# Two-layer graph network: the node update and the next layer's tables as one block pipeline, with centred features

## The chip, the cores and the metric

The kernel runs on one core of a Trainium2 chip. The metric is the device time of one launch in microseconds (us), the median of the runs made.

## The reference

A graph has 6250 nodes of 64 features and 200,000 edges sorted by destination. A first layer (L0) computes an attention over each node's incoming edges and a gated sum, adds it to x and normalises. Then a network of three layers runs. Cut to what matters:

```python
def _ln(x, g, b):
    m = x.mean(-1, keepdims=True)
    v = ((x - m) ** 2).mean(-1, keepdims=True)
    return (x - m) / jnp.sqrt(v + 1e-05) * g + b
...
edge_attr = _mlp(_ln(edge_embed, eng, enb), eW1, eb1, eW2, eb2)
for l in range(3):
    h = _ln(x, n1g[l], n1b[l])
    xi, xj = (h[dst], h[src])
    q = (xi @ Wq[l] + bq[l]).reshape(-1, H, HD)
    kn = (xj @ Wkn[l] + bkn[l]).reshape(-1, H, HD)
    ke = (edge_attr @ Wke[l] + bke[l]).reshape(-1, H, HD)
    ...                                      # vn, ve alike
    alpha = (q * (kn + ke)).sum(-1) / scale  # softmax over the edges of a node
    msg = ((vn + ve) * alpha[..., None]).reshape(-1, D)
    agg = jax.ops.segment_sum(msg, dst, num_segments=n)
    gate = jax.nn.sigmoid(agg @ Wih[l] + bih[l] + h @ Whh[l] + bhh[l])
    upd = agg + gate * (h @ Wself[l] + bself[l] - agg)
    x = x + upd @ Wout[l] + bout[l]
    h2 = _ln(x, n2g[l], n2b[l])
    x = x + _mlp(h2, mW1[l], mb1[l], mW2[l], mb2[l])
return _ln(x, ng, nb)
```

The result is added to the network's input and normalised once more, `_layernorm(x + ...)`. Of the next layer's h only the mean-free part of x is used; the last norm too takes the mean away.

## The kernel before, in words

All waits and orders are written out by hand: each engine has one program, and semaphores that the text names tie them. The stages follow each other in time:

- **Opening.** SP issues the loads. A loop over seven groups builds the node table `tab0`: SP loads features (`load_features`, L340), PE turns and multiplies (L645, L649), ACT copies, SP stores (`store_tables`, L402). POOL meanwhile gathers blocks of `dst` (L552), then gathers chunk 0 from `tab0` (L546), then scatters `s2exp` (L565).
- **First pass.** 28 chunks of 128 x 56 edges. POOL gathers 56 rows a chunk (L546) with one indirect DMA for each, in seven groups of eight; DVE runs the scans of L0's attention; PE and ACT run the edge network in seven steps a chunk, four 512-column products each way (L689, L696). From the second group on POOL holds until PE has finished a step of the chunk before (`m_pe`). ACT copies a chunk's states once a chunk (L910).
- **Tables of a layer (L728 to L745, L952, L1391 to L1412).** Node features lie turned, two nodes' 64 features on 128 partitions, in 3200 columns: six blocks of 512 columns and one of 128 (`BLK`, `NB` = 7). Each operation runs over all seven blocks before the next: mean (PE, L726), centre (DVE, L1379), square (ACT, L939), mean square (PE), Ln (L946) and Exp with scale -0.5 (L950), product and scale (L1384, L1387), projection (PE, L744) and biases (DVE, L1409 and L1411). SP stores `tabkv` block by block, then all of h and of the queries; POOL scatters the queries into `qexp`, 49 indirect DMAs of 128 nodes (L599), as soon as a block is ready.
- **Edge pass of a layer.** 28 chunks; POOL gathers keys and values (L546), 56 a chunk; DVE scans; ACT copies states to S1 and stores them.
- **Node update (L761 to L806, L992 to L1007, L1472 to L1519).** POOL fetches the final edge state of each node (L588, 49 DMAs). Blocks go in two halves (`HALVES`: blocks 0 to 2, then 3 to 6). In a half each operation runs over all its blocks before the next: `sums`, turn, copy, gate, self, mix, out, the second norm, four hidden products with Relu, the folded product, and the addition to x.
- **End.** The last two norms, operation by operation over all blocks, turned back and stored.

SP's queue between node update and tables: it waits for the end of the node update (L516), issues the 30 loads of the next layer's node weights (L457 to L469), stores x, then stores tables; then come source indices, edge features and the next table weights (L480 to L499). POOL's first gather of a layer waits for the indices (`idx1`), for `a_out` and for `h_out`.

## Time and profile before

| | us |
|---|---|
| runs (three) | 9158.19, 9160.3, 9160.95 |
| median | 9160.3 |
| profiled execution: its own time | 9160.98 |
| its span | 9159.2 |
| busy: PE, DVE, ACT, POOL | 3667.0, 5799.7, 2862.4, 6365.8 |

The span is the time from the first to the last instruction in the profile. Busy time is the sum of an engine's instructions; issuing a plain DMA and waiting are not counted. A row of waits says which engine stood still in front of which line, and what ended the wait.

### The profile page before, as it was taken

To read this page: it belongs to the slowest core of one execution; us is meant where nothing else is said; L and a number is where in the kernel's file an instruction comes from. 1 tells how busy PE (TensorE), PEld (TensorE's weight loads), DVE (VectorE), ACT (ScalarE), POOL (GpSimd) and SP (SyncE) were. 2 spreads that over 40 slices of the span, in tenths; PEclk is the share of its full clock that TensorE was granted. 3 is DMA by queue.
4 is the path that set the end of the run, shared out by engine and by line. 5 is a ranking of instruction groups with operands and counts; after the bars stand their busy time and mean duration, and the time that the engine had idled before them with its cause. 6 is when DMAs were issued, how large, how long until landed. Compare 5 with 4: busy or idle time off the path is not lost.

```text
span 9159.2 us, 45368 instructions
## 1 busy us (share of the span) xinstructions
PE 3667.0 (40%) x9857; PEld 2190.5 (24%) x9857; DVE 5799.7 (63%) x6114; ACT 2862.4 (31%) x2181; POOL 6365.8 (70%) x6734
## 2 busy tenths in 40 slices
PE   2677777776323233223342232322242222223325
PEld 1333333333122122212121221222222122212212
DVE  1666666666366776676437667767744776677673
ACT  0566666666122222222222222222221222222223
POOL 6677777774577777777457777777736777777762
PEclk9988888888656566555666665665576656656557
DMA  3455555554433443444234334434314443444331
GB/s 52 161 192 180 186 179 174 175 184 148 132 131 131 139 149 131 139 140 141 64 108 148 132 132 141 147 131 139 125 49 138 139 149 131 137 141 141 131 110 48
DMA packets 405487, 1247.08 MB, mean 136 GB/s; under 512 B 196101, under 2 KB 253910, under 8 KB 360006
## 3 DMA queue, kind: packets, MB, share of 16 engines
q0 software_dynamic: 215104, 429.19, 17.4%
q1 hardware_dynamic: 169606, 468.24, 14.6%
q10 hardware_dynamic: 20736, 349.23, 9.5%
q14 instruction: 31, 0.25, 0.0%
q8 instruction: 10, 0.16, 0.0%
HBM read 808.34 MB, written 437.84 MB: 136 GB/s over the span
## 4 chain that ended last, share of the span: by engine, by line
POOL 52%; issue 20%; PE 17%; ACT 7%; DVE 2%; DMA 1%; DVEq 1%; ACTq 0%; POOLq 0%; SPq 0%
POOL G L546 49%; PE PS L696 7%; PE PS L689 6%; ACT S L910 4%; POOL qexp L599 1%; PE PS L777 1%; POOL QQ L588 1%; PE PS L781 1%; ACT hid L886 1%; PE PS L666 1%; POOL s2exp L565 1%; POOL S L552 1%; POOL G L588 1%; ACT S L851 0%; ACT L855 0%
## 5 line engine op out<-in xcount | busy, mean ns | idle before, releaser
L546 POOL DMA_INDIRECT G<-tabkv,srcI x4704 | 4438.4, 944 | 1433.6 <-issue 1433.6
L756 PE MATMUL PS<-Wkvp,EA 128*128 128x256 f32 x4704 | 1672.9, 531 | 4296.3 <-DVE PX L1438 4217.8
L756 PEld LDWEIGHTS PS<-Wkvp,EA 128*128 128x128 f32 x4704 | 1253.4, 274 | 4716.5 <-DVE PX L1438 4381.7
L546 POOL DMA_INDIRECT G<-tab,srcI x1568 | 1481.4, 945 | 571.9 <-issue 507.2
L959 ACT ACTIVATE QQ<-QQ 128x3584 f32<-128x3584 f32 x84 | 538.4, 6410 | 3313.5 <-DVE PX L1438 3063.1
L1435 DVE TENSOR_TENSOR PS<-PS,G 128x512 f32<-128x512 f32 x588 | 408.4, 695 | 1593.3 <-DMA G<-tabkv,srcI 1575.3
L973 ACT ACTIVATE S<-SX 128x4480 f32<-128x4480 f32 x81 | 663.7, 8194 | 1238.4 <-DVEq L1462 1238.4
L689 PE MATMUL PS<-xT,W1p 128*128 128x512 f32 x1568 | 768.5, 636 | 252.2 <-ACT xT L847 243.1
L1424 DVE TENSOR_TENSOR_SCAN QQ<-PS,QQ 128x456 f32<-128x456 f32 x672 | 679.4, 1082 | 207.9 <-ACT QQ L959 192.3
L1461 DVE TENSOR_TENSOR_SCAN SX<-PS,SX 128x456 f32<-128x456 f32 x756 | 763.2, 1082 | 12.2
L696 PE MATMUL PS<-hid,W2p 128*128 128x512 f32 x1568 | 710.9, 596 | 34.2 <-ACT hid L886 31.5
L1438 DVE TENSOR_TENSOR PX<-PS,QQ 128x512 f32<-128x512 f32 x588 | 624.6, 1062 | 43.8
L886 ACT ACTIVATE hid<-PS,b1c 128x512 f32<-128x512 f32 x784 | 489.1, 684 | 300.6 <-PE PS L689 300.6
L1454 DVE TENSOR_TENSOR SX<-G,PS 128x3584 f32<-128x3584 f32 x84 | 525.7, 6258 | 87.8 <-ACT PS L968 87.8
L689 PEld LDWEIGHTS PS<-xT,W1p 128*128 128x128 f32 x1568 | 318.7, 205 | 660.4 <-issue 396.8
L1436 DVE TENSOR_TENSOR G<-PS,G 128x512 f32<-128x512 f32 x588 | 399.4, 679 | 0.0
L696 PEld LDWEIGHTS PS<-hid,W2p 128*128 128x128 f32 x1568 | 284.4, 190 | 342.0 <-issue 227.7
L910 ACT ACTIVATE S<-S 128x7336 f32<-128x7336 f32 x27 | 360.5, 13352 | 0.0
L599 POOL DMA_INDIRECT qexp<-PX,startI x147 | 140.9, 958 | 312.2 <-DVEq L1412 268.3
L1441 DVE TENSOR_REDUCE al<-PX 128x448 f32<-128x3584 f32 x84 | 326.6, 3888 | 7.7
L666 PE MATMUL PS<-ident,xe 128*128 128x128 f32 x784 | 132.0, 296 | 363.0 <-DVE xe L1188 363.0
L894 ACT ACTIVATE eaC<-PS,b2c 128x512 f32<-128x512 f32 x196 | 134.7, 687 | 418.8 <-PE PS L696 418.8
(311 smaller groups left out, 4090.8 us busy)
## 6 DMA issues: line engine op xcount, KB each, us to landing
st<-S ACTq DMA_DIRECT2D x81, 2240.0 KB, 7.8
EA<-eaT SPq DMA_DIRECT2D x84, 1792.0 KB, 7.8
QQ<-qexp SPq DMA_DIRECT2D x84, 1792.0 KB, 7.3
st<-S ACTq DMA_DIRECT2D x27, 3668.0 KB, 12.0
G<-tabkv,srcI POOLq DMA_INDIRECT x4704, 2.5
xe<-in_edge_attr SPq DMA_DIRECT2D x28, 1792.0 KB, 8.1
qexp<-zeros SPq DMA_DIRECT2D x28, 1792.0 KB, 12.6
eaT<-eaC ACTq DMA_DIRECT2D x28, 1792.0 KB
```

What stands on the lines that cost most here:

```text
L546: nc.gpsimd.indirect_dma_start(out=G[:, u, t, :], out_offset=None, in_=tab[:, :], in_offset=IND(ap=srcI[:, u, t:t + 1], axis=0)).then_inc( ...
L689: last = mm(PS[:, 1 + 2 * r + kh, :], W1p[:, r, kh, :], xT8[:, :], start=True, stop=True)
L696: last = mm(PS[:, 5, :], W2p[:, kh, r, :], hid8[:, r, kh, :], start=(r == 0 and kh == 0), stop=(r == 1 and kh == 1))
L756: last = mm(PS[:, b + j // 2, 2 * P * (j % 2):2 * P * (j % 2) + 2 * P], EA[:, u, 4 * s + j, :], Wkvp[:, :], start=True, stop=True)
L886: f(hid8[:, r, kh, :], PS[:, 1 + 2 * r + kh, :], ACT.Relu, bias=b1c[:, kh:kh + 1]).then_inc(m_act, 1)
L910: f(S0r[:, :, :], SY[:, :, 1:CX].rearrange("p r c -> p c r"), ACT.Copy).then_inc(s0_rows, 1)
L959: f(Qf[:, :, 1:CX], Q1.rearrange("p c d -> p d c"), ACT.Copy).then_inc(q_flat, 1)
L973: f(S1[:, :, :], SX[:, :, 1:CX].rearrange("p r c -> p c r"), ACT.Copy).then_inc(s_rows, 1)
L1424: scan(rows, gate8f, rows, 0.0, ALU.mult, ALU.add)
L1438: tt(PR[:, steps, :], kv_of(b)[:, :, 0:D], Qf[:, :, 1 + 8 * s:9 + 8 * s].rearrange("p d t -> p t d"), ALU.mult).then_inc(kv_used, 1)
L1454: tt(SX[:, 2 * H:R1, 1:CX].rearrange("p (j h) x -> p j h x", h=H), G1[:, u, :, D:2 * D].rearrange("p t (h d) -> p d h t", h=H), score8[:, ...
L1461: scan(rows, gate8f, rows, 0.0, ALU.mult, ALU.add)
```

## The change

The node update of a layer, the next layer's tables (or, after the last layer, the two last norms) become one list of steps. Each step has a position; block k's step of position d stands at 8k + d (`SKEW` = 8), and each engine issues its own steps in that order (`in_turn`). So several blocks are under way at once.

The features x are kept centred: x is centred once at the start with `Cmat` (identity minus the mean matrix), and `Wout`, `mW2` and their biases are centred once a layer (`centred_weights`), so that the sums stay mean-free, and the two mean products and centrings in each block's norms go. The inverse root, Ln and Exp on ACT, becomes Sqrt on ACT and a reciprocal on DVE (`scaled_by_spread`). The product of h with `Whh` is computed for all blocks ahead of the pipeline, and the gate product adds to it. Projections are done and handed over in quarters of a block.

On SP's queue the node weights of layer 0 and the weights of the last norm are loaded in the opening, before the loop that builds `tab0`; those of a later layer are loaded behind its table stores. h, x and the queries are stored block by block. `x1` is loaded for the end into S1. The layer loop runs twice, and the last layer is written out behind it. In the first pass POOL holds from the third group on, one step earlier.

```diff
+TILES = NPR
+SKEW = 8
+def in_turn(depth):
+    order = sorted((SKEW * k + d, k, step) for k in range(NB) for step, d in depth.items())
+    return [(k, step) for _, k, step in order if not (step.startswith("project") and int(step[-1]) * P >= BLK[k][1])]
...
+        NODE_PE = {"turn": 1, "gate": 3, "self": 5, "out": 7, "spread2": 10, "hidden0": 12, "hidden1": 14, "hidden2": 16,
+                   "hidden3": 18, "fold": 20}
+        NODE_ACT = {"agg": 2, "gate": 4, "square2": 9, "root2": 10.5, "relu0": 13, "relu1": 15, "relu2": 17, "relu3": 19}
+        NODE_DVE = {"sums": 0, "mix": 6, "onto": 8, "norm": 11, "onto2": 21}
+        TABLE_PE = {"spread": 23, "project0": 25, "project1": 25.5, "project2": 26.5, "project3": 27.5}
+        TABLE_ACT = {"square": 22, "root": 23.5}
+        TABLE_DVE = {"h": 24, "project0": 26, "project1": 26.5, "project2": 27.5, "project3": 28.5}
+        LAST_PE = {"spread": 23, "y_centre": 25, "y_spread": 27, "y_turn": 29}
+        LAST_ACT = {"square": 22, "root": 23.5, "y_square": 26, "y_root": 27.5}
+        LAST_DVE = {"y": 24, "y_norm": 28, "y_copy": 30}
+
+        def bank_of(k, j):
+            return k - 1 if k > 0 and j % 2 == 1 else k
...
             edge_weights(0)
             table_weights(0)
+            node_weights(0)
+            for q in range(2):
+                for j, name in ((NGC, "ng"), (NBC, "nb")):
+                    sp.dma_start(cb[q * D:(q + 1) * D, j:j + 1], A[name].unsqueeze(1), allow_slow_non_contiguous=True).then_inc(c_x, 16)
...
+            def store_tables1(m):
+
                 for k in range(NB):
-                    hold(sp, waits_sp, a_dve, l * A_DVE + 2 * NB + k + 1)
+                    hold(sp, waits_sp, projection_used, m * TILES + tiles_to(k))
...
+                if last:
+                    hold(sp, waits_sp, st1_out, (l + 1) * (16 * (NCH + 1)) + 16)
+                    sp.dma_start(nX1, x1Td[:, :]).then_inc(c_x, 16)
+                else:
+                    edge_weights(l + 1)
+                    store_tables1(l + 1)
+                    node_weights(l + 1)
...
-                        if k > 0:
-                            hold(pool, waits_pool, m_pe, 28 * (2 * i + u - 1) + (4 * k - 3 if k > 1 else 0))
+                        if k > 1:
+                            hold(pool, waits_pool, m_pe, 28 * (2 * i + u - 1) + (4 * k - 7 if k > 2 else 0))
...
+                    j = int(step[-1])
+                    if j == 0:
+                        hold(pe, waits_pe, h_ready, m * NB + k + 1)
+                    elif j == 1:
+                        hold(pe, waits_pe, projection_used, m * TILES + max(4 * k, 1))
+                    else:
+                        hold(pe, waits_pe, projection_used, m * TILES + 4 * k + (j - 1 if k > 0 else j))
+                    mm(PS[:, bank_of(k, j), 0:6 * D], nH[:, c0 + j * P:c0 + (j + 1) * P], Wqkv[:, :],
+                       start=True, stop=True).then_inc(projected, 1)
...
-                    f(nB4[:, c0:c0 + w], PS[:, k, 0:w], ACT.Ln, bias=epsc[:, 0:1]).then_inc(ln_ready, 1)
...
-                    f(nB4[:, c0:c0 + w], nB4[:, c0:c0 + w], ACT.Exp, scale=-0.5).then_inc(done, 1)
...
+            for k in range(NB):
+                c0, w = BLK[k]
+                act.wait_ge(x0_centred, k + 1)
+                f(nX[:, c0:c0 + w], PS[:, k, 0:w], ACT.Copy)
+                f(nB3[:, c0:c0 + w], PS[:, k, 0:w], ACT.Square).then_inc(squared, 1)
+            for k in range(NB):
+                root(k, 0)
...
+            def scaled_by_spread(k, dst, g_, b_):
+
+                c0, w = BLK[k]
+                cols = slice(c0, c0 + w)
+                v.reciprocal(nB4[:, cols], nB4[:, cols])
+                settle()
+                tt(nB5[:, cols], nX[:, cols], nB4[:, cols], ALU.mult)
+                settle()
+                return ts(dst[:, cols], nB5[:, cols], cb[:, g_:g_ + 1], cb[:, b_:b_ + 1], ALU.mult, ALU.add)
...
+                elif step == "y_norm":
+                    dve.wait_ge(y_rooted, k + 1)
+                    v.reciprocal(nB4[:, cols], nB4[:, cols])
```

## Rows read from the trace of the kernel before

**Rows 1.** Windows, one boundary: us, then busy PE, PEld, DVE, ACT, POOL, clock, DMA

```profile
4547.00:4651.00 104.00, 87.65 (x220) 41.11 (x220) 43.14 (x79) 46.41 (x75) 0.40 (x2) 0.90 0.06 20
...
sum 230.00, PE 128.04 PEld 62.44 DVE 71.28 ACT 59.51 POOL 96.22; mean PE 42.68 PEld 20.81 DVE 23.76 ACT 19.84 POOL 32.07
```

**Rows 2.** List of waits, whole span: us in total, times, longest

```profile
DVE PS L1435 <- DMA G<-tabkv,srcI: 1575.3, 252, 8.4
...
POOL qexp L599 <- DVEq L1412: 268.3, 3, 103.6
...
POOL G L546 <- PE PS L696: 57.8, 34, 17.1
```

**Rows 3.** Chain that ended last, in order of time: start, us, what

```profile
1340.88 13.26 ACT S L910
...
1413.41 13.28 ACT S L910
...
4471.95 4.08 DMA st<-S
...
4611.53 11.21 PE PS L781 x32
...
8943.84 4.08 DMA st<-S
```

**Rows 4.** Timeline at the first boundary: start, us, engine, line

```profile
4495.57 0.20 DVE L1483 TENSOR_SCALAR QQ<-QQ 128x64 f32<-128x64 f32 x1 [13.47 <-DMA QQ<-st,endI]
...
4497.72 1.09 PE L766 MATMUL PS<-ident,PX 128*128 128x128 f32 x4 [23.33 <-DVEq L1490]
...
4623.76 1.12 SPq L361 DMA_DIRECT2D cb<-in_bself  x2
...
4642.27 0.42 SPq L471 DMA_DIRECT2D xTd<-G  x1
...
4714.07 0.96 POOL L546 DMA_INDIRECT G<-tabkv,srcI  x1 [0.30 <-issue]
```

**Rows 5.** Opening: timeline, the table stores' line, and their landing

```profile
27.97 0.43 SPq L383 DMA_DIRECT2D bqkv<-in_bve  x1
...
35.84 0.40 SPq L340 DMA_DIRECT2D xe<-in_x  x1
...
95.69 0.94 POOL L546 DMA_INDIRECT G<-tab,srcI  x1 [0.30 <-issue]
...
L402 SPq DMA_DIRECT2D tab<-xe x7: 388/390/422, 41.4 to 88.0; - x7
...
tab<-xe SPq DMA_DIRECT2D x7, 458.5 KB, 4.5
```

**Rows 6.** Timeline of one chunk of the first pass

```profile
1355.57 0.23 DVE L1208 TENSOR_TENSOR al<-G,ewC 128x56 f32<-128x56 f32 x1
...
1366.06 0.94 POOL L546 DMA_INDIRECT G<-tab,srcI  x1 [2.84 <-PE PS L696]
```

**Rows 7.** DVE groups by form, 4484 to 4672: busy us, mean ns, idle before

```profile
L1379 DVE TENSOR_TENSOR EA<-G,PS 128x512 f32<-128x512 f32 x12 | 7.7, 682 | 0.6 <-PE PS L726 0.5
...
L1485 DVE RECIPROCAL QQ<-QQ 128x64 f32<-128x64 f32 x6 | 3.3, 552 | 0.4
...
L1387 DVE TENSOR_SCALAR EA<-EA,cb 128x512 f32<-128x512 f32 x6 | 3.3, 546 | 0.5
...
L1485 DVE RECIPROCAL QQ<-QQ 128x8 f32<-128x8 f32 x1 | 0.2, 202 | 0.1
```

**Rows 8.** A table load by form (mean ns); PE's busy time and clock

```profile
L946 ACT ACT_TABLE_LOAD x3 | 3.8, 1283 | 0.1
...
9117.00:9122.00 5.00, 0.16 (x2) 0.99 0.00 0
9122.00:9127.00 5.00, 4.31 (x5) 0.50 0.01 2
```

**Rows 9.** POOL's query scatters: duration ns, first and last start

```profile
L599 POOL DMA_INDIRECT qexp<-PX,startI x147: 954/958/986, 2414.6 to 6947.3; - x147
```

More of the change, by code:

```diff
@@ L747, in _, with edges1 @@
+            def edges1(l):
+                hold(pe, waits_pe, projection_used, (l + 1) * TILES)
                 with pe.Fori(0, NCH // 2) as i:
@@ new lines, in _ @@
+            pe.wait_ge(a_x, 16)
+            hold(pe, waits_pe, l_t, 16 * NTW)
+            for k in range(NB):
+                c0, w = BLK[k]
+                mm(PS[:, k, 0:w], Cmat[:, :], nX[:, c0:c0 + w], start=True, stop=True).then_inc(x0_centred, 1)
+            for k, step in in_turn(TABLE_PE):
+                table(k, step, 0)
+            with pe.Fori(0, L - 1) as l:
+                edges1(l)
+                hold(pe, waits_pe, l_t, (l + 2) * (16 * NTW))
+                for k, step in in_turn({**NODE_PE, **TABLE_PE}):
+                    if step in NODE_PE:
+                        node(k, step, l)
+                    else:
+                        table(k, step, l + 1)
@@ new lines, in _ @@
+            edges1(L - 1)
+            for k, step in in_turn({**NODE_PE, **LAST_PE}):
+                c0, w = BLK[k]
+                if step in NODE_PE:
+                    node(k, step, L - 1)
+                elif step == "spread":
+                    table(k, step, L)
+                elif step == "y_centre":
+                    pe.wait_ge(h_ready, L * NB + k + 1)
+                    mm(PS[:, k, 0:w], Cmat[:, :], nB5[:, c0:c0 + w], start=True, stop=True).then_inc(y_centred, 1)
+                elif step == "y_spread":
+                    pe.wait_ge(y_squared, k + 1)
+                    mm(PS[:, k, 0:w], onesD[:, :], nB3[:, c0:c0 + w], start=True, stop=True).then_inc(y_spread, 1)
+                else:
+                    pe.wait_ge(y_normed, k + 1)
+                    for j in range(w // P):
+                        last = tr(PS[:, k, j * P:(j + 1) * P], nB5[:, c0 + j * P:c0 + (j + 1) * P], ident[:, :])
+                    last.then_inc(y_turned, 1)
@@ new lines, in square, with root @@
+            def square(k, m):
+                c0, w = BLK[k]
+                act.wait_ge(x2_ready, (m - 1) * NB + k + 1)
+                f(nB3[:, c0:c0 + w], nX[:, c0:c0 + w], ACT.Square).then_inc(squared, 1)
+            def root(k, m):
+                c0, w = BLK[k]
+                act.wait_ge(spread, m * NB + k + 1)
+                f(nB4[:, c0:c0 + w], PS[:, k, 0:w], ACT.Sqrt, bias=epsc[:, 0:1]).then_inc(rooted, 1)
+            for k in range(NB):
+                c0, w = BLK[k]
+                act.wait_ge(x0_centred, k + 1)
+                f(nX[:, c0:c0 + w], PS[:, k, 0:w], ACT.Copy)
+                f(nB3[:, c0:c0 + w], PS[:, k, 0:w], ACT.Square).then_inc(squared, 1)
@@ L955, in query, with layer @@
+            for k in range(NB):
+                root(k, 0)
+            def layer(l):
                 def query(n):
@@ L1413, in _, with layer @@
+            biases(0)
+            for k, step in in_turn(TABLE_DVE):
+                table(k, step, 0)
+            def layer(l):
                 v.memset(gate8[:, :, 0:1], 0.0)
@@ L1492, in mix @@
-                def mix(k, c0, w):
-                    stt(nB4[:, c0:c0 + w], PS[:, k, 0:w], cb[:, BSELF:BSELF + 1], nB2[:, c0:c0 + w], ALU.add, ALU.subtract)
+                centred_weights(l)
+            with dve.Fori(0, L - 1) as l:
+                layer(l)
+                biases(l + 1)
+                for k, step in in_turn({**NODE_DVE, **TABLE_DVE}):
+                    if step in NODE_DVE:
+                        node(k, step, l)
+                    else:
+                        table(k, step, l + 1)
```

446 lines of the change are left out of this document (221 added, 225 removed).

## The prediction

> **What bounds the kernel now.** I read the windows by stage first [rows 1]. At the boundary between two layers POOL first fetches the 49 groups of final edge states; from 4547 to 4651 it then does nothing (0.40 us busy) while PE is busy 88 of 104 us; and up to 4714 it scatters the 49 query groups. The list of waits names the hole: POOL waited three times, 268 us in all and 104 us at the longest, for the DVE step that ends the first table block (L1412) [rows 2]. Once the first attention gather is out at 4714, POOL issues without a pause, and DVE waits for it; so the start of the gathers sets the end of each layer's edge pass. Layers repeat every 2236 us (8943.84 against 4471.95) [rows 3]. What the change can win at the two boundaries between layers is therefore an earlier first gather than 4714.07 [rows 4]; at the end of the program, an earlier last block; in the opening, where the chain that ended last runs through one POOL issue after another, every microsecond that POOL starts later is lost [rows 5].
>
> In the first pass one chunk takes 72.5 us (one L910 to the next) [rows 3]. POOL's 56 gathers at 1.25 us take 70 and then POOL waits: 2.84 us in the chunk shown, 57.8 us over the pass, always for PE [rows 6, 2].
>
> **The first pass.** The released group goes out 8 gathers, 10 us, earlier, and the next group then waits for the same product. DVE uses the gathered rows at 1355.57 after waiting for ACT (L910), not for a gather [rows 6], and no wait of DVE on a gather of this pass is in the list. PE and ACT set the 72.5 us. Cost 0, bounds -3 and +3 (other DMA traffic beside them). The work that hides it is that PE and ACT chain; without it POOL's wait of at most 58 us would be the price.
>
> **The opening.** 30 loads of node weights and 4 of the last norm move ahead of the feature loop on SP's queue. SP is idle from 28.4 to 35.8 [rows 5]. In the old place the 30 take 18.5 us (4623.76 to 4642.27) [rows 4]; 4 more make 21, so SP is free at about 49.5 and not before 35.84. The table stores ran from 41.4 to 88.0 and landed 4.5 us later, 92.5; the first gather at 95.69 waited for nothing [rows 5], a slack of 3. Shifting the second feature load by 13.6 and following the loop's hand-overs (load lands, turn, product, store, landing), the last store shifts by 9.5 to 11, so the gather starts 7 us late. Bounds 3 and 13. Also one DVE subtraction of 128 columns before the one-hot sums, 0.2. I take +7.
>
> **Table stage 0.** ACT now copies and squares all seven blocks from PSUM, loads one table (1.28) [rows 8] and takes roots; DVE then needs a reciprocal, a product and a scale. The Exp pass over all blocks and its own table load are gone. Block 0 is ready at about 2409.6 against 2414.6 [rows 9]; DVE then needs 9 us a block against POOL's 10.1 us for eight scatters, so POOL stays the bound and keeps those 5 us. I take -5, bounds -8 and +3.
>
> **The reciprocal** is the largest added work: Exp(-0.5 Ln) on ACT becomes Sqrt on ACT and a reciprocal of up to 512 columns on DVE. The trace has none wider than 64: 202 ns for 8 columns, 552 for 64 [rows 7], a slope of 6.25 ns a column. Linearly a block costs 0.55 + 448 x 0.00625 = 3.35 us; scaled in proportion it costs 8 x 0.552 = 4.4. I take 3.35, since the two rows show a fixed part, and keep 4.4 for the range. The Trainium skill (VectorE: DVE Perf Modes, on why there are eight slices) says the reciprocal iterates with a repeat count of 8; an estimate from that is 4.3 us plus the fixed part for a block, the upper of the two ends. By it the sum would be some 45 us worse; the two rows' slope is below it, so I don't take it.
>
> **DVE's load.** At a boundary it did 71 us [rows 1]. Two centrings a block go (12 x 0.68 = 8 us) [rows 7], two reciprocals come (6.25 block equivalents x 2 x 3.35 = 42), and projection goes in quarters, 8 small additions a block for 4 (+4, my estimate): 109 us, 17.4 a block and with the added drains 18.5. PE: 16 products (each two records) over three blocks of 512 columns and one of 128 in 11.21 us [rows 3]: 0.86 us for 512 columns at full clock. Each block keeps 13 such, four projections (2.6) and four turns (0.9): 14.6 us. ACT was busy 59.5 us a boundary [rows 1], 9.5 a block, and loses more than it gains: not the bound. It loads a table twice a window, because Sigmoid (position 4) lies between the roots (10.5 and 23.5, that is 2.5 and 7.5 of a window). The Trainium skill (ScalarE: Activation LUTs, the table of advice) says to do all functions of one table set before switching and gives about 2.7 us a load; the row says 1.28 [rows 8]. By 2.7 each window would grow by up to 3 us; the row decides.
>
> **The pipeline's window.** Engines run in order, so I walked the written order (8 positions a window) with these durations. In a full window DVE does h of block k-3 (3.35, a drain of 0.08, product and drain 0.77, scale 0.55 [rows 7]: 4.75), onto, sums (2.15: 4495.57 to PE's turn at 4497.72 [rows 4]): 7.6. Then PE turns block k (1.1), projects, and spreads block k-1, which ends at 11.2; root at 11.95; DVE's second norm to 16.75; two quarters and onto2 to 19.0; mix to 21.2; and the next window's root, behind square, spread and a table load, is done at 22.3. So DVE works 18.5 of 22.3, and what it waits for is the turn and spread in front of the second norm and the root at the window's end. PE stands still about 4.3 us, works 0.7, and stands 2.1 more before the turn. After a stillness of 5.1 us its granted clock went from 0.99 to 0.50 for the next 5 us [rows 8], which would add 2.1 to the path; I take 1.5, hence 23.8, bounds 18.6 (DVE's work alone) and 29 (PE's 14.6 at half clock).
>
> **A boundary.** The first sums start at 4495.57 as before. The first three windows, when a block's 24 dependent steps pass one by one, take 12.5, 17 and 17, and 4 for the slow clock: 50, to 4545.6. Then 27 (block 0's projections all share one bank), 24, 24, 22, 17, 9 and 5: the last block is ready at about 4673.5. Rows come every 10.2 us, faster than windows, so they hide; POOL's eight scatters (10.1) also fit a window, and the last ones end near 4681. What is late next is SP: only after the last block's four stores (1.9) does it issue the 30 node weights (18.5), and behind these stand the source indices (2.4 with landing), which POOL's first gather waits for. 4673.5 + 22.8 = 4696.3 against 4714.07: -17.7 each, -35 for two. The 19 table weights and the query load stand behind on SP, some 11 us after the first gather, hidden by DVE's waits for gathers (1575 us in 252 waits [rows 2]). If that cover were gone: 11 us a layer. Bounds of a boundary: -49 with windows of 18.6, +16 with windows of 30.
>
> **The end.** The first sums come at 4495.57 + 4471.9 = 8967.5. Windows hold y (5.5), the second norm (4.75) and y_norm (4.1), whose reciprocals all stand in one chain (y, centre, square, spread, root, y_norm, turn, then self and mix): 26.8, with clock 28. 8967.5 + 50 + 28 + 28 + 28 + 25 + 18 + 13.5 + 8.5 = 9166.5, and 2.8 for the last store: 9169.3 against 9159.2, +10. Bounds -27 and +50. Covers: loads of x1 and the last norm are done before the sums.
>
> **Sum.** 7 + 0 - 5 - 35 + 10 = -23. The profiled run took 9160.98 with a span of 9159.2, and the median is 9160.3, so the forecast is 9137.
>
> **Rivals.**
> *The clock holds* and the waits overlap as the order intends: 1.5 off each window and 4 off each fill: about -30 a boundary and -2 at the end: 7 - 5 - 60 - 2 = -60, 9100. For it: with PE busy 84% of the time the clock was 0.90 [rows 1]. Against it: the stillness of 5.1 us [rows 8]. If windows shrink to DVE's own 18.6 it would be 7 - 5 - 98 - 27 = -123, 9037; against that speaks the chain walked above.
> *The reciprocal costs 4.4*, the other side: 2.1 more a window, five and a half windows at each boundary, 3.2 in some six at the end, 45 us in all: +22, 9182. It decides from windows 1.5 us longer than I take (25.3): 15 of them eat the 23. Unseen hand-overs of that size do the same.
> *PE becomes the bound at half clock*: 29 us of products a block; boundaries +16, end +50: +84, 9244. Against it: PE busy 84% had a clock of 0.90 [rows 1], and a PE that lags is busy throughout.
> *The change doesn't bring the gathers forward*, because SP's weights stand before the indices: that is already in the sum at 18.5; without it 9100.
>
> **Chances.** Forecast's own case 0.38, its range 9115 to 9160; clock holds 0.20; windows near DVE's work 0.10; reciprocal or hand-overs dearer 0.22; PE at half clock 0.10. About 0.2%, 18 us, is what this measurement can tell from no change. Faster: 0.30 and 0.24 of the first case, 0.54; within: 0.14 and half of the fourth, 0.25; slower 0.21. The range leaves out PE at half clock (0.10), half of the windows near DVE's work (0.05) and the worst of the fourth case (0.05): 9070 to 9195. It holds 9100 and 9182, so both signs.
>
> **What would show it.** The new reciprocals' mean for 512 columns (3.35). First gather of the chunks at about 102.5, of a layer at about 2480 and 4700, and what it waits for: SP's indices, not scatters. First sums to last projection 178 us. SP's node weights right behind the last block's stores. Clock in the windows 0.7 to 0.9. First-pass chunk 72.5 us with POOL still waiting 2.8. Wrong would make it: windows outside 22 to 26 us, or an opening that moves by other than 7.

## The result and the profile after

The changed kernel takes 9175.6 us (median of 20 runs, 9171.3 to 9180.0), the kernel before 9161.0 beside it (20 runs): a ratio of 1.0016, 95% interval 1.001 to 1.0022. The forecast was 23 us faster; it is 15 us slower, and the interval leaves no doubt of the sign, though the time is inside the range of 9070 to 9195. The profiled run has a span of 9171.6 us, 12.4 more than before.

Where the 12.4 us come from is read off the chain that ended last (start, us, what): the last state store of each edge pass ends a stretch.

```profile
2282.90 5.76 DMA st<-S
...
4480.90 4.08 DMA st<-S
...
6710.41 4.11 DMA st<-S
...
8938.50 4.09 DMA st<-S
```

Two of the same rows of before stand in [rows 3], the other two are:

```profile
2276.39 5.82 DMA st<-S
...
6708.12 4.10 DMA st<-S
```

The differences:

| stretch | before | after | change | forecast |
|---|---|---|---|---|
| opening and first pass | 2276.4 | 2282.9 | +6.5 | +7 |
| table stage 0 and layer 0's edge pass | 2195.6 | 2198.0 | +2.4 | -5 |
| boundary 1 and layer 1's edge pass | 2236.2 | 2229.5 | -6.7 | -17.7 |
| boundary 2 and layer 2's edge pass | 2235.7 | 2228.1 | -7.6 | -17.7 |
| last node stage and norms | 215.4 | 233.1 | +17.7 | +10 |

**The opening**, in the timeline (start, us, engine, line, what it waited for); it answers to the first gather of [rows 5]:

```profile
102.96 0.94 POOL L593 DMA_INDIRECT G<-tab,srcI  x1 [7.38 <-DMA tab<-xe]
```

POOL starts 7.3 us later and now waits for the stores of the first table. From there to the last state store it takes 2179.9 us, before 2180.7: the first pass neither gains nor loses.

**Table stage 0**, timeline of the first two blocks:

```profile
2400.31 3.35 DVE L1461 RECIPROCAL EA<-EA 128x512 f32<-128x512 f32 x1 [14.89 <-ACT EA L1018]
...
2405.20 1.62 PE L818 MATMUL PS<-Wqkv,G 128*128 128x384 f32 x2 [6.36 <-DVE G L1465]
...
2413.97 1.91 PE L809 MATMUL PS<-G,onesD 128*128 128x512 f32 x2
...
2415.72 0.99 POOL L646 DMA_INDIRECT qexp<-PX,startI  x1 [55.69 <-DVEq L1516]
2415.93 0.69 ACT L1018 ACTIVATE EA<-PS,epsc 128x512 f32<-128x512 f32 x1 [15.65 <-PE PS L809]
2416.65 3.35 DVE L1461 RECIPROCAL EA<-EA 128x512 f32<-128x512 f32 x1 [1.80 <-ACT EA L1018]
...
2427.68 0.96 POOL L646 DMA_INDIRECT qexp<-PX,startI  x1 [2.12 <-DVEq L1516]
```

The first scatter is 5.4 us earlier in its stretch than before ([rows 9]: 2414.6 - 2276.4 against 2415.7 - 2282.9). But block 1's variance product (L809) stands in PE's queue behind block 0's four projections, so its root comes only at 2415.93, and the next blocks follow every 11 to 12 us, not every 10.1. POOL waits 1 to 2.3 us before each of them, and its first gather of the layer comes 204.0 us after the state store, not 201.4.

**The first boundary.** What is ready when is read off POOL's waits for the last quarter of each block (timeline; in brackets POOL's idle time):

```profile
4577.45 0.98 POOL L646 DMA_INDIRECT qexp<-PX,startI  x1 [21.76 <-DVEq L1516]
4607.07 0.96 POOL L646 DMA_INDIRECT qexp<-PX,startI  x1 [19.78 <-DVEq L1516]
4631.53 0.96 POOL L646 DMA_INDIRECT qexp<-PX,startI  x1 [14.47 <-DVEq L1516]
4652.95 0.95 POOL L646 DMA_INDIRECT qexp<-PX,startI  x1 [11.45 <-DVEq L1516]
4671.03 0.95 POOL L646 DMA_INDIRECT qexp<-PX,startI  x1 [8.11 <-DVEq L1516]
4686.88 0.95 POOL L646 DMA_INDIRECT qexp<-PX,startI  x1 [6.07 <-DVEq L1516]
```

Its start, one full window and its end:

```profile
4502.64 0.56 PE L840 MATMUL PS<-cb,Cmat 128*128 128x2 f32 x2 [19.31 <-DMA G<-xTd]
...
4504.51 0.25 DVE L1475 TENSOR_SCALAR QQ<-QQ 128x64 f32<-128x64 f32 x1 [0.66 <-DMA QQ<-st,endI]
...
4510.36 0.60 PE L776 MATMUL PS<-ident,PX 128*128 128x128 f32 x4
...
4511.73 1.10 PE L780 MATMUL PS<-G,Wn 128*128 128x512 f32 x2 [0.78 <-ACT G L993]
...
4586.24 3.35 DVE L1461 RECIPROCAL EA<-EA 128x512 f32<-128x512 f32 x1 [1.53 <-ACT EA L1018]
...
4593.88 1.09 PE L776 MATMUL PS<-ident,PX 128*128 128x128 f32 x4 [1.87 <-DVEq L1482]
...
4596.04 1.91 PE L801 MATMUL PS<-EA,mW1s 128*128 128x512 f32 x2
...
4597.74 1.62 PE L789 MATMUL PS<-G,onesD 128*128 128x512 f32 x2
...
4610.84 3.35 DVE L1461 RECIPROCAL EA<-EA 128x512 f32<-128x512 f32 x1 [1.53 <-ACT EA L1018]
...
4691.07 0.28 DVE L1515 TENSOR_TENSOR PX<-PS,bqkv 128x128 f32<-128x128 f32 x1
...
4693.94 1.11 SPq L392 DMA_DIRECT2D cb<-in_bself  x2
...
4713.70 0.35 SPq L522 DMA_DIRECT2D srcI<-in_src  x1
...
4716.37 0.96 POOL L593 DMA_INDIRECT G<-tabkv,srcI  x1 [17.14 <-DMA srcI<-in_src]
```

From one h to the same step of the next block it is 24.6 us; in it PE's products cost double after its stillness (1.91 for 512 columns, 1.02 later), and the windows (us; busy PE, PEld, DVE, ACT, POOL; granted clock; DMA share, GB/s) say that DVE works 16.8 of the 24.6 us:

```profile
4586.20:4610.80 24.60, 17.86 (x39) 7.65 (x38) 16.78 (x22) 9.12 (x13) 3.92 (x4) 0.86 0.15 40
```

After the last block SP issues the node weights from 4693.9 on, then the source indices at 4713.70, and POOL has waited 17 us for them. That part of the forecast holds. The reciprocal's own line (duration min/median/max):

```profile
L1461 DVE RECIPROCAL EA<-EA x49: 953/3353/3355, 2400.3 to 9162.6; 128x512 f32<-128x512 f32 x42, 128x128 f32<-128x128 f32 x7
```

3.35 us for 512 columns, the slope of the two narrow rows of [rows 7].

### The profile page after: what moved, and what is told of

It reads as the page before. It is cut to its first block, busy times and chain, and to the rows that moved or that the text cites. A ratio compares the mean times of both kernels' runs of the same rounds, so it can differ in the third digit from the quotient of the medians.

```text
span 9171.6 us, 44763 instructions
## 1 busy us (share of the span) xinstructions
PE 3660.6 (40%) x9779; PEld 2159.1 (24%) x9779; DVE 5951.5 (65%) x6211; ACT 2909.8 (32%) x2189; POOL 6367.4 (69%) x6734
## 4 chain that ended last, share of the span: by engine, by line
POOL 50%; issue 19%; PE 17%; ACT 7%; DVE 4%; DMA 1%; SPq 1%; DVEq 1%; ACTq 0%; POOLq 0%
POOL G L593 49%; PE PS L743 7%; PE PS L736 6%; ACT S L964 4%; DVE EA L1461 1%; PE PS L818 1%; PE PS L801 1%; ACT hid L940 1%; PE PS L713 1%; POOL s2exp L612 1%; POOL G L635 1%; ACT S L905 0%; ACT L909 0%; DMA G<-xTd 0%; PE PS L793 0%
## 5 line engine op out<-in xcount | busy, mean ns | idle before, releaser
L833 PE MATMUL PS<-Wkvp,EA 128*128 128x256 f32 x4704 | 1633.4, 520 | 4239.4 <-DVE PX L1575 4163.4
L833 PEld LDWEIGHTS PS<-Wkvp,EA 128*128 128x128 f32 x4704 | 1222.3, 267 | 4651.5 <-DVE PX L1575 4333.8
```

The costliest lines, as they stand in the source:

```text
L833: last = mm(PS[:, b + j // 2, 2 * P * (j % 2):2 * P * (j % 2) + 2 * P], EA[:, u, 4 * s + j, :], Wkvp[:, :], start=True, stop=True)
```

## Experiments

All medians stand beside runs of the kernel before on the same chip; changes in us are against the changed kernel's 9175.6 unless said otherwise. "Stretch" is the time between two of the state stores above, in the profiled run. Of the small steps, three (the opening, the variance product, the two banks) have ratios whose intervals overlap with the interval of the kernel they vary: there the trace carries the argument, and the size in the median is uncertain by some us.

### The opening alone

```diff
             table_weights(0)
-            node_weights(0)
...
             sp.wait_ge(a_x, 16)
+            node_weights(0)
```

> The changed kernel with the 30 node weights and the 4 loads of the last norm issued where the table stage begins (after x has landed) and not in the opening. Theory: they hold SP's second feature load back, so POOL's first gather comes at 103 and not at 96; everything behind it in the first pass is a chain of POOL, PE and ACT, so the time falls by those 6.5 us, to 9169, and SP is free again at about 2411, before the first table block is ready at 2415. Rival: the first pass swallows a late start (it is not bound by POOL alone), and the time stays at 9175.6 within 2 us. Second rival: in the new place they stand ahead of the first block's stores and cost there what they give back: first gather of the first layer later by up to 10 us, time 9169 to 9180.

Measured: 9167.9 (ratio 1.0007, 0.9998 to 1.0016), 7.7 less; in the profiled run the first stretch is 5.3 shorter. The first gather is back:

```profile
95.90 0.94 POOL L593 DMA_INDIRECT G<-tab,srcI  x1 [0.30 <-issue]
```

The opening's term was right, in size and in mechanism, and the new place costs nothing: the next stretch is 2198.1 us, 2198.0 in the changed kernel.

### The first pass's gathers alone, on the kernel before

```diff
-                        if k > 0:
-                            hold(pool, waits_pool, m_pe, 28 * (2 * i + u - 1) + (4 * k - 3 if k > 1 else 0))
+                        if k > 1:
+                            hold(pool, waits_pool, m_pe, 28 * (2 * i + u - 1) + (4 * k - 7 if k > 2 else 0))
```

> The kernel before with one part of the change alone: the gathers of the first pass are released one step of the product further ahead. Theory: PE and ACT set the 72.5 us of a chunk, POOL waits for PE anyway, so nothing: 9161 within 3 us. Rival: the earlier gathers give back POOL's waits of 57.8 us or part of them (9105 to 9155), or crowd the other transfers of the pass (9165 or more).

Measured: 9160.4 against 9160.4 (ratio 1.000, 0.999 to 1.0009). Nothing, as forecast.

### Table stage 0: variance product ahead

```diff
-            for k, step in in_turn(TABLE_PE):
+            for k, step in in_turn({**TABLE_PE, "spread": 16}):
```

> The changed kernel, in the first table stage alone: PE does the variance product of block k+1 before the projections of block k and not behind them. Theory: the root of the next block stands behind the four projections, so a block takes 11.4 to 12.1 us where POOL's eight scatters take 10.1; with the product ahead DVE never waits for a root and POOL goes from block to block without a pause: waits of 2.1, 1.9, 1.2, 1.0 and 2.3 us go, about 7 in all, and the time falls by 5 to 8 us, to 9169. Rival: DVE's own work and the four projections that share a bank (2.5 us each at the lower clock) set the period, then the time falls by less than 2 us.

Measured: 9166.2 (ratio 1.0007, 0.9998 to 1.0016), 9.5 less; in the profiled run the stretch falls from 2198.0 to 2192.2, 5.8 less, and POOL's waits fall to at most 1.1 us. The whole profiled span is only 3.7 shorter. So the 5 us that the forecast had here existed; a place in PE's queue took them.

### Source indices ahead of the node weights

```diff
                 for u in range(2):
                     queries(u)
+                node_weights(l)
...
                     store_tables1(l + 1)
-                    node_weights(l + 1)
```

> The changed kernel with each layer's 30 node weights issued on SP behind that layer's first two query loads (so neither in the opening nor between the last table block and the source indices); the four loads of the last norm go where the table stage begins. Theory: at a boundary POOL's first gather waits 17 us for source indices that stand behind 18.9 us of weights; with the indices in front, POOL waits for its own scatters and the fetch of the boundary queries, which end at about 217 us after the last state store, and the gathers start at 218 to 220 and not at 234: 15 to 17 us at each of two boundaries, and the opening's 7.7 on top: 9175.6 - 7.7 - 32 = 9136. Rival: the weights now stand before the third chunk's indices, or the query load (14 us behind the first gather already) becomes what DVE waits for; then DVE starts as late as before, and less than 8 us a boundary is kept: 9152 to 9168.

Measured: 9139.2 (ratio 0.9976, 0.9966 to 0.9986), 36.4 less. The boundary stretches fall by 16.9 and 13.4, as much as the first gather moves (from 235.5 and 234.0 us after the last state store to 218.4 and 220.6); the rest is the opening. POOL goes from its last scatter through the boundary queries to the gathers without a wait. The query load is issued only at 4708.13, 14 us behind the first gather, and costs nothing, since the stretch shrinks as much as the gather moves:

```profile
4690.01 0.35 SPq L521 DMA_DIRECT2D srcI<-in_src  x1
...
4692.56 0.99 POOL L648 DMA_INDIRECT qb<-tabq,firstI  x1 [0.30 <-issue]
...
4693.85 0.97 POOL L592 DMA_INDIRECT G<-tabkv,srcI  x1 [0.30 <-issue]
```

So the node weights on SP's queue (18.9 us here, 18.5 in the sum) are a real price and an avoidable one, and without them the change is faster than the kernel before.

### The products with Whh inside each gate step

```diff
-                    mm(... Wn[:, 1, :], nB2[:, cols], start=False, stop=True ...)
+                    mm(... Wn[:, 2, :], nH[:, cols], start=True, stop=False)
+                    mm(... Wn[:, 1, :], nB2[:, cols], start=False, stop=True)
...
-                for k in range(NB):
-                    mm(PS[:, k, 0:w], Wn[:, 2, :], nH[:, c0:c0 + w], start=True, stop=False, ...)
```

> The changed kernel with the product of h and Whh back in each block's gate step (two products in a row), and the wait for the reloaded h and x in front of the first of them and no longer in front of the bias product. Theory: at each of the three node stages the first turn waited for 7.4 us of products that themselves waited for the reload; now the first sums are no longer held up by the copy of the bias (about 1 us) and the turn follows them at once: first turn 3.7 us earlier, the last block too, 3.7 us at each of two boundaries and at the end: -11, 9165. Rival: the added product in every window lies on the path (turn, project, spread) at 0.9 to 1.9 us and eats this: 0 to +10 us, 9176 to 9186.

Measured: 9174.8 (ratio 1.0016, 1.0007 to 1.0025), 0.8 less. The first turn did come earlier, and the gain was gone three rows later:

```profile
4504.66 1.09 PE L776 MATMUL PS<-ident,PX 128*128 128x128 f32 x4 [22.87 <-DVEq L1481]
...
4506.80 2.05 PE L782 MATMUL PS<-G,Wn 128*128 128x512 f32 x2 [1.05 <-ACT G L992]
4508.64 1.91 PE L783 MATMUL PS<-G,Wn 128*128 128x512 f32 x2
```

The seven products in front had left PE at full clock (the gate product of block 0 took 1.10); without them turn, gate and self each run at the lower clock, beside the added product. My theory, that the late first turn costs each stage 3.7 us, falls: the second norm of block 0 starts 45.9 us after the state store here and 45.2 in the changed kernel.

### Block 0's projections in two banks

On the run just told: its last bank stays unused until late, so block 0 can alternate.

```diff
-            return k - 1 if k > 0 and j % 2 == 1 else k
+            return (k - 1) % NB if j % 2 == 1 else k
```

> The changed kernel with the gate's two products in a row (as in the run of that part), which leaves the last block's PSUM bank unused until late, and block 0's second and fourth projection in that bank, so that block 0 alternates two banks as the others do. Theory: the step from block 0 ready to block 1 ready took 29.6 us where the later ones take 24.5 and I had 24; it is the four projections one after another through one bank (2.4 us each), and with two banks 5 us go at each boundary, 2 in the first table stage and 3 at most at the end, which has no projections: 9174.8 less 12: 9163. Rival: block 1's window is long for another reason (its turn and root pass while three blocks still fill the pipeline), and the time stays within 3 us of 9174.8.

Measured: 9174.4, but where the kernel before takes 9171.9: ratio 1.0003 (0.9994 to 1.0012), 0.13% or 12 us below the ratio of the run it builds on, with intervals that overlap. In the traces the first gathers of the two boundaries come 7.1 and 4.3 us earlier after the state store than in that run. The step from block 0 to block 1:

```profile
4577.90 0.99 POOL L646 DMA_INDIRECT qexp<-PX,startI  x1 [20.85 <-DVEq L1513]
4602.22 0.96 POOL L646 DMA_INDIRECT qexp<-PX,startI  x1 [13.85 <-DVEq L1513]
```

24.3 us, where the changed kernel has 29.6 and the run this one builds on 29.0. What the one bank costs is not only that its four projections pass one by one at the lower clock. In the changed kernel DVE's addition that frees it stands behind a second norm:

```profile
4569.18 3.35 DVE L1461 RECIPROCAL EA<-EA 128x512 f32<-128x512 f32 x1 [3.44 <-ACT EA L1002]
...
4574.65 1.23 PE L818 MATMUL PS<-Wqkv,G 128*128 128x384 f32 x2 [4.72 <-DVEq L1516]
...
4580.69 0.75 DVE L1498 SCALAR_TENSOR_TENSOR G<-PS,cbc,G 128x512 f32<-128x512 f32 x1 [4.16 <-PE PS L793]
```

PE stands still 4.7 us before block 0's fourth projection, the folded product behind it (L793) is late, and DVE then waits 4.2 us for that. With two banks neither wait is there, and from h of block 0 to h of block 1 it is 24.8 us in place of 31.1 (30.5 in the run it builds on).

### The load of x1 at the end

```diff
+                    sp.wait_ge(rows_got[3], (L + 1) * 128)
                     sp.dma_start(nX1, x1Td[:, :]).then_inc(c_x, 16)
...
-            dve.wait_ge(c_x, 80)
...
                 elif step == "y":
+                    if k == 0:
+                        dve.wait_ge(c_x, 80)
```

> The changed kernel, at the end of the program alone: the load of x1 (11.5 us) is issued only after 32 of the 49 groups of final states have been fetched, and DVE waits for it before the first y and no longer before the first sums. Theory: at the end the first sums come 26.8 us after the last state store, at the boundaries 23.6; the difference is this load, so 3 us come back: 9172.5. Rival: the later load is missed by y of block 0 (78 us after the last state store) or the 3 us are taken up by the first windows: 9175 or more.

Measured: 9176.7 (ratio 1.0017, 1.0008 to 1.0026), no gain. The first sums came 23.8 us after the last state store and not 26.8, but the first turn stayed at 29.9: PE comes to it at 8971.47, straight from the products with Whh that it began at 8963.95, so it waits for those and not for the sums. The theory falls; the late sums were real and covered.

### Without the wide reciprocals

```diff
-                v.reciprocal(nB4[:, cols], nB4[:, cols])
-                settle()
                 tt(nB5[:, cols], nX[:, cols], nB4[:, cols], ALU.mult)
```

> The changed kernel without the wide reciprocals of the layer's two norms and of the first last norm (what they should have turned into a factor is multiplied as it is; 41 of the 48 wide reciprocals and their drains are left out, those of y_norm stay). It prices the reciprocal by what its absence gives back. Theory: both stand in the chain of a window (h, turn, spread, root, norm), so a window of 24.6 us loses 2 x 3.4 and takes 18: 5.5 windows a boundary, 35 to 40 us each, 35 to 45 at the end, 10 or less in the first table stage, in all -110 to -130: 9045 to 9065. Rival: PE's 14.6 us at full clock (up to 22 at a lower one) and ACT's table loads take over as the bound, and less than 60 us come back: above 9115.

This leaves out the 42 wide and 7 narrow reciprocals of L1461. Measured: 9038.8 (ratio 0.9865, 0.985 to 0.988), 136.8 less; its four runs lie between 9033.9 and 9049.7. The profiled one is the longest of them, and there the boundaries are 35.9 and 32.7 shorter, the end 49.1, the table stage 6.5. At the first boundary blocks follow every 18.4 to 18.9 us, 6 less than 24.6 for 6.7 us of reciprocals left out. They stand in the chain almost whole.

### PE kept busy while DVE forms h

```diff
                     if j == 0:
+                        hold(pe, waits_pe, rooted, m * NB + k + 1)
+                        for _ in range(4):
+                            mm(PS[:, k, 0:w], onesD[:, :], nB3[:, c0:c0 + w], start=True, stop=True)
                         hold(pe, waits_pe, h_ready, m * NB + k + 1)
```

> The changed kernel with four more products of 512 columns in front of each block's first projection, where PE stands still while DVE forms h (their result is overwritten; nothing is left out). Theory: PE's stillness of 4.3 us lets the granted clock fall, and turn, projection, hidden product and variance product behind it then take twice as long (1.09, 1.49, 1.91 and 1.62 us); kept busy, PE runs them at full clock and a window loses 2 to 3 us: 5.5 windows at each of two boundaries: 22 to 33 us less, 9143 to 9154 (the end has no projections and no added products). Rival: the clock is no term of the window, or the 3.4 us of added products get in the way of turn and variance product: the same time within 5 us, or up to 20 more.

Measured: 9167.0 where the kernel before takes 9171.9: ratio 0.9994 (0.9985 to 1.0003), 0.22% or 20 us below the changed kernel's ratio. The full window, from h to h:

```profile
4583.60:4605.70 22.10, 18.82 (x48) 7.87 (x46) 16.79 (x23) 9.13 (x12) 4.50 (x5) 1.00 0.17 46
```

Here the granted clock is 1.00 in place of 0.86 and the window 22.1 in place of 24.6, with more work in it. The added products do not hold the clock everywhere: of the two such full windows at each boundary, one has it lower all the same.

```profile
4605.70:4631.00 25.30, 21.68 (x48) 9.32 (x46) 16.84 (x23) 9.13 (x12) 7.85 (x8) 0.87 0.21 62
...
6811.10:6836.00 24.90, 21.65 (x48) 9.31 (x46) 16.79 (x22) 9.13 (x12) 3.53 (x4) 0.86 0.15 39
6836.00:6858.50 22.50, 18.80 (x47) 7.88 (x46) 16.84 (x22) 9.12 (x12) 7.85 (x8) 1.00 0.24 70
```

With the same instructions a window takes 22.1 and 22.5 us at 1.00, and 25.3 and 24.9 at 0.87 and 0.86: the lower clock costs 2.4 to 3.2 us of a full window; I had taken 1.5. More of the gain comes at the end of the pipeline: the two steps from h to h after 4656.72 take 18.4 and 12.7 us in the changed kernel at a clock of 0.81 and 0.73, here 15.8 and 11.0 at 1.00. The start gives some of it back (h of block 0 comes 1.8 and 1.6 us later), and the last quarter comes 5.9 and 3.3 us earlier after the state store than in the changed kernel. In the table stage, where the same products stand, POOL waits once, for 0.8 us, and the first gather comes 196.1 us after the state store in place of 204.0 (stretch 2194.2 for 2198.0).

### Another order in the window

```diff
-        NODE_PE = {"turn": 1, ..., "spread2": 10, ...}
-        NODE_ACT = {"agg": 2, ..., "square2": 9, "root2": 10.5, ...}
-        NODE_DVE = {"sums": 0, "mix": 6, "onto": 8, "norm": 11, "onto2": 21}
+        NODE_PE = {"turn": 0.5, ..., "spread2": 8.8, ...}
+        NODE_ACT = {"agg": 0.7, ..., "square2": 8.3, "root2": 8.95, ...}
+        NODE_DVE = {"sums": -0.6, "mix": 6, "onto": 7.8, "norm": 9.5, "onto2": 21}
```

> The changed kernel with another written order inside the window: DVE does sums and onto before h of the block three behind (then the second norm before the quarters), PE turns and spreads before the projections, ACT squares, copies and takes the root before the relu. Nothing is added or left out. Theory: the window of 24.6 us is a chain (h 4.75 us on DVE, then turn and variance product on PE at the lower clock, then root, then the second norm), not DVE's work of 18.5; with sums covering the output product and h covering turn, spread and root, a window takes 19 to 20.5 us. Five and a half windows a boundary: 22 to 28 us each, and some 20 at the end, so 9100 to 9115 in all. Rival: PE at the lower clock (29 us a block) or ACT's two table loads set the window; then it stays above 23 and the time falls by less than 20 us.

Measured: 9124.3 (ratio 0.9962, 0.9949 to 0.9976), 51.4 less with the same instructions. The boundaries gain 10.9 and 10.5, less than expected, the end 26.9. h and the second norm now follow each other without a wait (timeline), and the window is 22.6 us at a clock of 0.92:

```profile
4579.74 3.34 DVE L1461 RECIPROCAL EA<-EA 128x512 f32<-128x512 f32 x1
...
4584.39 3.34 DVE L1461 RECIPROCAL EA<-EA 128x512 f32<-128x512 f32 x1
...
4602.37 3.34 DVE L1461 RECIPROCAL EA<-EA 128x512 f32<-128x512 f32 x1
```

```profile
4579.70:4602.30 22.60, 17.01 (x40) 7.27 (x38) 16.74 (x23) 8.90 (x12) 7.69 (x8) 0.92 0.24 70
```

The window of the changed kernel was a chain and not DVE's work, as the forecast had walked it; what the forecast did not draw from its walk is that another written order would shorten the chain.

### The three parts together, and variants

The order above, the indices first and the variance product ahead:

> The changed kernel with three of the parts above together: source indices ahead of the node weights (which also clears the opening), the first table stage's variance product ahead of the projections, and the new order inside the window. Theory: they sit in different places (SP's queue, the first table stage, the windows), so their gains add: 36.4 and 9.5 and 51.4 us off 9175.6, 9078. Rival: they share a bound. With blocks ready earlier POOL's own scatters (10.1 us for eight) and the fetch of the boundary queries end last, or the query load that stands behind the gathers is missed; then a boundary keeps less than 20 of its 27 us and the time is 9090 to 9110.

Measured: 9088.5 (ratio 0.9922, 0.9909 to 0.9936), 87 less than the changed kernel where the medians add to 97. The profiled spans add nearly exactly: 33.7, 3.7 and 49.2 off 9171.6 is 9085.0, measured 9086.7. The median lies between the theory's 9078 and the rival's 9090; the boundaries keep 24.6 and 23.1 us.

With a second order (gate, self and mix beside h and the norm, fold earlier, sums and two quarters later):

```diff
+        NODE_PE = {"turn": 0.5, "gate": 0.9, "self": 1.45, "out": 2.5, "spread2": 8.8, "hidden0": 10.45, ..., "fold": 18.4}
+        NODE_DVE = {"sums": -4, "mix": 2.05, "onto": 6, "norm": 9.5, "onto2": 19}
+        TABLE_DVE = {"h": 24, "project0": 26, "project1": 26.5, "project2": 28.2, "project3": 28.4}
```

> As the run with the three parts together, with a second written order of the window: gate and self of the new block and then mix stand beside h and the second norm, fold comes right behind hidden3, sums and the last two quarters behind onto2. Nothing is added or left out. Theory: in the window of 22.6 us DVE still waited 2.8 us for fold, 1.3 for out, 1.0 for self and about 2 for quarters; with the order walked through by durations DVE has one wait of 1 to 2 us left and a window takes 18.5 to 20. 2.6 to 4 us off some 17 windows: 45 to 65 us less than the other run. Rival: PE, in order too, now waits for DVE in front of products that were ready (self and out behind the projections), and the window does not get shorter: within 15 us of the other run, or slower.

Measured: 9113.9 (ratio 0.9948, 0.9935 to 0.9962), 25 more than the run with the three parts. Both theories saw half: blocks follow every 18.6 to 20.9 us and not 20.2 to 24.1, but the first is ready 103.7 us after the state store and not 93.2, and the end takes 239.7 us and not 207.6. The boundary stretches are 1.3 and 3.9 us shorter, so the whole loss is at the end.

With the factors formed on ACT as before the change:

```diff
-                f(nB4[...], PS[:, k, 0:w], ACT.Sqrt, bias=epsc[:, 0:1]).then_inc(rooted, 1)
+                f(nB4[...], PS[:, k, 0:w], ACT.Ln, bias=epsc[:, 0:1]).then_inc(ln1, 1)
+                act.wait_ge(ln1, m * NB + k + 1)
+                f(nB4[...], nB4[...], ACT.Exp, scale=-0.5).then_inc(rooted, 1)
```

> As the run with the three parts together, with the factor of the layer's two norms and of the first last norm formed by ACT as before the change (Ln, then Exp of -0.5 times it) and not by Sqrt on ACT and a reciprocal on DVE; 41 wide reciprocals go, 41 passes of 0.58 us and some 80 table loads of 1.28 us more come on ACT. Theory: DVE's 6.9 us of reciprocals set the window; ACT was busy 8.9 us of 22.6 and has room for 3.7 more, so a window takes 17 to 19 us: 60 to 80 us less than the run with the three parts. Rival: ACT's four loads a window stand in the chain (root, then norm; square, root, then h), and the window only falls by what DVE gains less 3.7: 2 to 3 us, 30 to 50 us less; or nothing if ACT's in-order queue holds the relus up.

Measured: 9067.6 (ratio 0.99, 0.9885 to 0.9915), 21 less than the three parts, less than either the theory (60 to 80) or the rival's 30 to 50. Window and clock:

```profile
4580.00:4600.30 20.30, 15.55 (x40) 6.41 (x39) 10.26 (x20) 13.89 (x17) 7.69 (x8) 1.00 0.27 78
```

DVE works only 10.3 us of 20.3; ACT now works 13.9, with five table loads of 1.28 us among it, and DVE waits for it (3.6 us before the second norm's product). This is the best version run that leaves nothing out: 1.0% faster than the kernel before, 1.2% faster than the changed one. So of the parts of the change, putting Sqrt and a reciprocal in place of Ln and Exp is one that costs, once the order is mended: the four runs without it (9061.5 to 9070.3) all lie below the five of the three parts (9088.5 to 9089.3).

The second order at the boundaries alone, on this version:

> As the run with Ln and Exp on ACT, with the second written order at the two boundaries alone; the end keeps the first one, since the second made the end 32 us longer. Theory: at the boundaries the second order gave windows of 20 and not 22.6 us, but a start 10 us later, and 2 to 5 us less in all; with DVE's reciprocals gone DVE has nothing left that this order could hide, so a boundary gets at most 3 us shorter or up to 8 longer: 9062 to 9084 in all. Rival: the order's earlier fold takes away the 2.8 us for which DVE waits in each window and each boundary gets 10 us or more shorter: 9045 or less.

> The same kernel as the run with the second order at the boundaries and Ln and Exp on ACT, once more, beside the next two: the first time it ran where the kernel before took 10879 us. The expectations stand: theory 9062 to 9084; rival 9045 or less.

Measured first: 10694.9, where the kernel before took 10879.2 (ratio 0.9831, 0.9817 to 0.9844). Then, on another chip: 9121.1 where the kernel before took 9171.9 (ratio 0.9945, 0.9931 to 0.9958), some 40 us above the version it varies. A boundary stretch takes 2216 and 2219 us, not 2193 and 2194; the first blocks follow every 23.5 to 25.6 us there (19.6 to 21.3 in the version, first boundary), and the first comes 11 us late. Both expectations fall: with the reciprocals on DVE this order was 1 to 4 us a boundary better, and without them it is some 20 us worse (first gather 218.1 and 220.7 us after the state store, 198.8 and 200.1 in the version). Which of its steps is the late one was not taken apart.

## Why the prediction was wrong

**Right in size and mechanism:** the first pass (0), the opening (+6.5 for +7), the reciprocal (3.353 us for 3.35), SP's weights in front of the indices, and that the window is a chain with DVE's work and waits in it. That its length came out so near (24.6 for 23.8) is partly luck: DVE works 16.8 us of it and not 18.5, and waits 7.8 and not 5.3. An estimate from what the Trainium skill states of the reciprocal (VectorE: DVE Perf Modes, the passage on eight slices: a repeat count of 8, by estimate 4.3 us a block and a fixed part) is contradicted by the 42 wide rows, median 3353 ns. The rivals with a reciprocal of 4.4 us and with PE as the bound did not come true. Nearest is the second half of the first of them, unseen hand-overs, but they did not lengthen the full windows to 25.3: they sat in the table stage and at the two ends of the pipeline.

**Wrong, term by term** (35 us in all, against the span):

1. *Table stage 0, 7.4 us.* The failing step is "DVE then needs 9 us a block against POOL's 10.1 us, so POOL stays the bound". The durations were right; the variance product of the next block stood behind four projections on PE. The run with it ahead gives 5.8 of the 7.4 back.
2. *The boundaries, 11.0 and 10.1 us.* At the first, ready times after the first sums, forecast against measured: block 0 at 77 and 72.9, block 1 at 101 and 102.6, then 125 and 127.0, 147 and 148.4, 164 and 166.5, 173 and 182.4, and the end at 178 and 186.8. The start was 4.1 us too long, which hid part of what follows. Two steps failed. In "27 (block 0's projections all share one bank), 24" the shared bank was seen but priced at 3 us, on block 0; it also held up PE's queue behind DVE's second norm, and the step to block 1 is 29.6. Two banks bring it to 24.3. And the drain, the last blocks, behind which no new ones start ("17, 9 and 5"), is 18.1, 15.9 and 4.5, the largest error of this sum: block 5's last steps do not shrink to 9 us when block 6 is short. That is so with two banks too (17.3, 14.9 and 4.7). Part of it is the clock, which the forecast had in the first and the full windows and not in the drain: PE is busy 12.1 us of the 18.4 from h of block 4 to h of block 5 and is granted 0.81, and where the added products kept the clock at 1.00 the three steps took 15.7, 13.7 and 4.6. The rest, some 5 us of the step for 9, no run takes apart. Another 2.2 us are SP's: 25.0 us from the last quarter to the first gather, for the 22.8 in the sum.
3. *The end, 7.7 us.* The first sums came 3.2 us late, which the run with the later load showed to be covered. From them the first output block is copied after 71.5 us, where the forecast had 78; the next follow after 29.1, 27.6, 26.2, 21.6, 20.5 and 7.5 us, for "28 + 28 + 25 + 18 + 13.5 + 8.5". So the windows were right here and the start was overestimated; what failed is the drain again, by 10.6 us in two blocks. No run takes it apart further, and its cause at the end stays open.

**The clock.** Its term, 1.5 us a window, was too small by some 1 to 1.7: the run with the added products shows 2.4 to 3.2. It is part of the 24.6 for 23.8. The wait that I did not have in the sum at all, the reload of h and x and seven products before the first turn, costs nothing on balance: those products also bring PE to full clock, which the run without them has to pay for.

So the change does what the forecast said at the boundaries, at two fifths of the size, and it gave back elsewhere more than it won: 6.5 us in the opening and 17.7 at the end against 14.3 at the boundaries, and 2.4 in the table stage. Three placements (indices first, the variance product ahead, another order in the window) recover 87 us.

## What to carry to other kernels

When a stage is a pipeline of blocks on engines that run in order, the written order is a cost of its own: write down for every in-order queue, SP's too, what stands in front of the step on the critical path, since the same instructions in another order were worth 51 us here, and thirty small loads in front of one index load 13 to 17 us a boundary. Price the ends of the pipeline apart from its windows: the first block's shared bank and the last blocks' chain were the two largest errors at a boundary, while the full windows were right within 1 us. And test an order again whenever a duration in it changes.

## What was unexpected

*More work, less time.* Four added products of 512 columns a block (some 3.6 us of PE each time) made the kernel some 20 us faster; what changed beside them, in half of the full windows and in the drain, is the granted clock, 1.00 for 0.73 to 0.86, and with it the length of the other products.

*Chips differ.* The kernel before took 9159.6 to 9161.0 us in most comparisons, 9171.9 in one and 10879 in one. The same variant ran beside both of the last two, so it can be compared: the engines' busy times are alike (POOL 6377.6 us where the kernel before took 10879, 6383.0 on the other chip), but what the DMA engines move per second is not, as the first part and the DMA line of the slow run's page show:

```profile
PE 3710.8 (35%) x9779; PEld 2157.7 (20%) x9779; DVE 5800.0 (54%) x6162; ACT 2993.5 (28%) x2283; POOL 6377.6 (60%) x6734
...
DMA packets 409122, 1246.80 MB, mean 117 GB/s; under 512 B 195125, under 2 KB 253702, under 8 KB 364406
```

The same bytes moved at a mean of 137 GB/s on the other chip. The extra time is in waits, and the profile names no cause for many of them (27% of the chain that ended last is put down to "another core or an unknown queue"). Each chip was used at one time only, so whether it was the chip or the hour is not shown. The same variant's ratio was 0.9831 there and 0.9945 on the other: even a ratio taken on one chip does not carry over to a chip as slow as this.
